# Gated cross-attention and feed-forward on one core: two head pairs per attention step in place of one

## What is computed

```python
def xattn(x, context):                      # x is layer-normed before
    q = split_heads(x @ Wq) * 64 ** -0.5
    k, v = map(split_heads, split(context @ Wkv))
    k, v = concat(null_kv[0], k), concat(null_kv[1], v)   # one null key, value
    out = merge_heads(softmax(q @ k.T) @ v) @ Wout
    return layernorm(out, eps=1e-6) * ln_scale + ln_bias
x = x + tanh(g_xattn) * xattn(layernorm(x), ctx)
x = x + tanh(g_ffn) * ffn(layernorm(x))     # gated, quantised over whole tensors
```

## Time and profile before

| what | value |
|---|---|
| median of three executions | 598.54 us |
| the profiled execution, its own time | 599.63 us |
| its span in the trace | 597.6 us |
| busy: PE, PE's weight loads, DVE, ACT, POOL | 524.0, 456.4, 410.5, 298.4, 123.6 us |
| group 0, and each of groups 1 to 5 | 50.10 us |
| group 6 | 42.01 us |
| group 7, to the start of its W | 33.16 us |
| from the end of W to the end of the kernel | 166.2 us |

### The profile page before, as it was taken

One profiled execution on the slowest core, in us unless ns is written; L12 is line 12 of the kernel. 1 busy time (PEld: TensorE's weight loads), 2 busy tenths in 40 slices (PEclk: granted clock), 3 DMA queues, 4 the chain that ended last, 5 costly groups with the idle time before them and its releaser, 6 DMA issues. The chain is left out here.

```text
span 597.6 us, 10965 instructions
## 1 busy us (share of the span) xinstructions
PE 524.0 (88%) x3921; PEld 456.4 (76%) x3921; DVE 410.5 (69%) x1077; ACT 298.4 (50%) x858; POOL 123.6 (21%) x137
## 2 busy tenths in 40 slices
PE   2999999999999999999999999997639999500997
PEld 2988889888988988888898898885528888400996
DVE  4779744754764574575476458658748989999685
ACT  3635532632542362363254335327325569897773
POOL 3001301220221130122022112213031029900000
PEclk9999999999999999999999999999959999855799
DMA  7922001101100110110110001005001000100033
GB/s 257 361 88 72 1 1 54 37 1 54 35 0 0 53 35 0 53 35 0 35 45 8 1 2 36 2 1 160 0 19 35 2 0 1 35 1 1 1 106 105
DMA packets 18478, 25.86 MB, mean 43 GB/s; under 512 B 1216, under 2 KB 15808, under 8 KB 18448
## 3 DMA queue, kind: packets, MB, share of 16 engines
q1 hardware_dynamic: 18192, 25.17, 12.8%
q0 software_dynamic: 256, 0.30, 0.2%
HBM read 21.27 MB, written 4.19 MB: 43 GB/s over the span
## 5 line engine op out<-in xcount | busy, mean ns | idle before, releaser
L804 ACT ACTIVATE probs<-bank,nmax 128x129 f32<-128x129 f32 x256 | 90.9, 368 | 117.8 <-DVE nmax L1132 117.7
L1551 POOL TENSOR_TENSOR probs<-probs,rinv 128x512 f32<-128x512 f32 x64 | 66.7, 1042 | 337.8 <-DVE rinv L1140 337.8
L607 PE MATMUL bank<-wv,ctxT 128*128 128x512 f32 x384 | 94.2, 397 | 0.0
L599 PE MATMUL bank<-ctxT,wk 128*128 128x256 f32 x672 | 88.9, 282 | 0.0
L599 PEld LDWEIGHTS bank<-ctxT,wk 128*128 128x128 f32 x672 | 83.6, 188 | 0.0
L607 PEld LDWEIGHTS bank<-wv,ctxT 128*128 128x128 f32 x384 | 70.5, 188 | 16.9 <-issue 1.2
L1144 DVE COPY pT<-bank 128x512 f32<-128x512 f32 x64 | 43.7, 682 | 20.7 <-PE bank L670 18.7
L599 PE MATMUL bank<-xnT,wq 128*128 128x256 f32 x336 | 54.7, 298 | 0.0
L785 ACT ACTIVATE oT<-bank 128x256 fp32r<-128x256 f32 x64 | 24.7, 386 | 60.0 <-PE bank L679 60.0
L804 ACT ACTIVATION_READ_ACCUMULATOR probs<-bank,nmax 128x1 f32 x256 | 52.0, 203 | 0.0
L599 PEld LDWEIGHTS bank<-xnT,wq 128*128 128x128 f32 x336 | 43.2, 188 | 7.2 <-issue 1.2
(11 more groups left out here) (170 smaller groups left out, 810.6 us busy)
## 6 DMA issues: line engine op xcount, KB each, us to landing
craw<-in_ctx SPq DMA_DIRECT2D x8, 512.0 KB, 3.3
stage<-in_L_xattn_Wkv SPq DMA_DIRECT2D x8, 512.0 KB, 11.9
xa<-in_x SPq DMA_DIRECT2D x8, 256.0 KB, 2.7
xr<-in_x SPq DMA_DIRECT2D x8, 256.0 KB, 2.8
x_scratch<-y SPq DMA_DIRECT2D x7, 256.0 KB, 2.1
x2all<-x_scratch SPq DMA_DIRECT2D x1, 1792.0 KB, 8.3
xres<-x_scratch SPq DMA_DIRECT2D x6, 256.0 KB, 2.8
out<-yout SPq DMA_DIRECT2D x6, 256.0 KB, 2.2
```

What stands on the lines that cost most here:

```text
L599: last = mm(bk[:, n * TG:(n + 1) * TG], wt[a][:, k, f], act_t[b][:, k, :], start=(k == 0 and i == 0), stop=(k == kk - 1 and i == len(TERMS ...
L607: last = mm(bk[:, :], ctxT[a][:, k, b * S:(b + 1) * S], wv[w][:, k, h * 512:(h + 1) * 512], start=(k == 0 and i == 0), stop=(k == KC - 1 a ...
L804: last = nc.scalar.activation(probs[:, c % 2, u, 0:NK], score_bank[c % 2][h][:, b * QW:b * QW + NK], ACT.Exp, bias=nmax[:, c % 2, u:u + 1] ...
L1551: G.tensor_tensor(probs[:, c % 2, :, 0:S], probs[:, c % 2, :, 0:S], rinv[:, c % 2, :].rearrange("p (u o) -> p u o", o=1).to_broadcast([P, ...
```

## The change

The eight steps become four (PAIRS = NS // 2), each with two head pairs 2p and 2p+1.

- PE: scores of both head pairs of the next step stand back to back at its head, in all four score banks; then prob_transposes(2p), the units of plan step 2p, prob_transposes(2p+1), the units of plan step 2p+1, and then the values of both, into all 512 columns of pv_bank. In the last group the second scores stand ahead of prob_transposes(2p+1).
- out_high and out_low take 512 columns at once, once in a step.
- DVE: both maxima stand at the head of the step; then for each head pair the other work (now beside(c)), prob_copy, inverse_sums, unit evacuations; out_low at the end of the step. attention_stats no longer has a maxima in its middle.
- ACT: exps of one head pair ahead of each of the two sets of unit evacuations, out_high at the end.
- The prologue makes scores, maxima and exps of head pairs 0 and 1 of group 0; POOL normalises two there.
- ot_lo and pv_done count steps of two (g * PAIRS + p).

```diff
--- before.py
+++ after.py
@@ -642,7 +643,7 @@
                         o = bank[0][:, 0:D] if last_group and b else bk[:, b * D:(b + 1) * D]
                         mm(o, mean[:, :], wc[:, :], start=True, stop=False)
                         if b == 0:
-                            wait(pe, ot_lo, g * NS + NS)
+                            wait(pe, ot_lo, g * PAIRS + PAIRS)
                         for k in range(KF):
                             for i, (a, w) in enumerate(TERMS):
                                 last = mm(o, oT[a][:, k, b * S:(b + 1) * S], wout[w][:, k, :],
@@ -670,14 +671,16 @@
                     last = nc.tensor.transpose(pt_bank[:, u * P:(u + 1) * P], probs[:, c % 2, u, 0:S], ident[:, :])
                 last.then_inc(pt_done, 1)
 
-            def values(g, c):
-                wait(pe, pt_copied, g * NS + c + 1)
-                wait(pe, ot_lo, g * NS + c)
-                for b in range(GB):
-                    for h in range(2):
-                        rows = slice(h * DH, (h + 1) * DH)
-                        last = mm(pv_bank[rows, b * S:(b + 1) * S], v[:, b, c, rows],
-                                  pT[:, c % 2, 2 * h + b, :], start=True, stop=True)
+            def values(g, p):
+                wait(pe, pt_copied, g * NS + 2 * p + 2)
+                wait(pe, ot_lo, g * PAIRS + p)
+                for n in range(2):
+                    c = 2 * p + n
+                    for b in range(GB):
+                        for h in range(2):
+                            rows = slice(h * DH, (h + 1) * DH)
+                            last = mm(pv_bank[rows, n * TG + b * S:n * TG + (b + 1) * S], v[:, b, c, rows],
+                                      pT[:, n, 2 * h + b, :], start=True, stop=True)
                 last.then_inc(pv_done, 1)
 
             for pos in range(len(PRO)):
@@ -685,22 +688,25 @@
                 if PRO[pos] == "k6":
                     pe.wait_ge(null_ready, 1)
                     scores(0, 0)
+                    scores(0, 1)
 
             def group(g):
                 final = isinstance(g, int) and g == NG - 1
                 pos, (steps, tail) = 0, plan(g)
-                for c in range(NS):
-                    if c + 1 < NS:
-                        scores(g, c + 1)
-                    for _ in steps[c]:
-                        unit(g, pos)
-                        pos += 1
-                    prob_transposes(g, c)
-                    if c:
-                        values(g, c - 1)
-                if not final:
-                    scores(g + 1, 0)
-                values(g, NS - 1)
+                for p in range(PAIRS):
+                    to = (g, 2 * p + 2) if p + 1 < PAIRS else (None if final else (g + 1, 0))
+                    if to:
+                        scores(to[0], to[1])
+                        if not final:
+                            scores(to[0], to[1] + 1)
+                    for n in range(2):
+                        if n and to and final:
+                            scores(to[0], to[1] + 1)
+                        prob_transposes(g, 2 * p + n)
+                        for _ in steps[2 * p + n]:
+                            unit(g, pos)
+                            pos += 1
+                    values(g, p)
                 for u in tail:
                     if u != "C":
                         unit(g, pos)
@@ -806,9 +812,10 @@
                                                 bias=nmax[:, c % 2, u:u + 1], accum_out=rowsum[:, c % 2, u:u + 1])
                 last.then_inc(exp_done, 1)
 
-            def out_high(g, c):
-                wait(act, pv_done, g * NS + c + 1)
-                high(oT[0][:, c, :], pv_bank[:, 0:TG]).then_inc(ot_hi, 1)
+            def out_high(g, p):
+                wait(act, pv_done, g * PAIRS + p + 1)
+                high(oT[0][:, 2 * p:2 * p + 2, :],
+                     pv_bank[:, :].rearrange("p (c s) -> p c s", c=2)).then_inc(ot_hi, 1)
 
             def ctx_high(n, units_before):
                 act.wait_ge(ctx_in, (n + 1) * 16)
@@ -831,6 +838,7 @@
                 split("pro", npos[0])
                 if PRO[npos[0]] == "k6":
                     exps(0, 0)
+                    exps(0, 1)
                 if PRO[npos[0]] == "V11":
                     ctx_high(1, PRO.index("V11") + 1)
                 npos[0] += 1
@@ -838,21 +846,15 @@
             def group(g):
                 final = isinstance(g, int) and g == NG - 1
                 pos, (steps, tail) = 0, plan(g)
-                for c in range(NS):
-
-                    weights = steps[c][0][0:1] == "F"
-                    if c + 1 < NS and not weights:
-                        exps(g, c + 1)
-                    for _ in steps[c]:
-                        split(g, pos)
-                        pos += 1
-                    if c + 1 < NS and weights:
-                        exps(g, c + 1)
-                    if c:
-                        out_high(g, c - 1)
-                if not final:
-                    exps(g + 1, 0)
-                out_high(g, NS - 1)
+                for p in range(PAIRS):
+                    to = (g, 2 * p + 2) if p + 1 < PAIRS else (None if final else (g + 1, 0))
+                    for n in range(2):
+                        if to:
+                            exps(to[0], to[1] + n)
+                        for _ in steps[2 * p + n]:
+                            split(g, pos)
+                            pos += 1
+                    out_high(g, p)
                 for u in tail:
                     if u == "C":
                         ctx_high(g + 2, units(g)[1] + BODY.index("V11") + 1)
@@ -1078,7 +1080,6 @@
                 for b in range(GB):
                     last = V.bn_stats(bn[:, 2 + b, :], bk[:, b * D:(b + 1) * D])
                 ln2.count(last)
-                maxima(g + 1, 1)
                 ln2.wait()
                 settle()
                 for b in range(GB):
@@ -1144,9 +1145,10 @@
                 V.tensor_copy(pT[:, c % 2, :, :],
                               pt_bank[:, :].rearrange("p (u s) -> p u s", u=4)).then_inc(pt_copied, 1)
 
-            def out_low(g, c):
-                dve.wait_ge(ot_hi, g * NS + c + 1)
-                low(oT[1][:, c, :], pv_bank[:, 0:TG], oT[0][:, c, :]).then_inc(ot_lo, 1)
+            def out_low(g, p):
+                dve.wait_ge(ot_hi, g * PAIRS + p + 1)
+                low(oT[1][:, 2 * p:2 * p + 2, :], pv_bank[:, :].rearrange("p (c s) -> p c s", c=2),
+                    oT[0][:, 2 * p:2 * p + 2, :]).then_inc(ot_lo, 1)
 
             def weight_scales(m):
 
@@ -1202,8 +1204,10 @@
             while npos[0] < len(PRO):
                 if PRO[npos[0]] == "V00":
                     ln_stats(1)
+                    inverse_sums(0, 0)
                 elif PRO[npos[0]] == "V10":
                     ln_rstd()
+                    inverse_sums(0, 1)
                 elif PRO[npos[0]] == "V01":
                     ln_apply()
                 elif PRO[npos[0]] == "V11":
@@ -1213,21 +1217,18 @@
                 split("pro", npos[0])
                 if PRO[npos[0]] == "k6":
                     maxima(0, 0)
-                    inverse_sums(0, 0)
+                    maxima(0, 1)
                 if PRO[npos[0]] == "V11":
                     ctx_low(1)
                 npos[0] += 1
 
-            maxima(0, 1)
             dve.wait_ge(const_ready, 1)
 
             def group(g):
                 peeled, final = isinstance(g, int), isinstance(g, int) and g == NG - 1
                 first = peeled and g == 0
                 pos, (steps, tail) = 0, plan(g)
-                for c in range(NS):
-                    if 1 <= c < NS - 1:
-                        maxima(g, c + 1)
+                def beside(c):
 
                     if c == 1 and not first:
                         attention_rstd(g - 1)
@@ -1247,25 +1248,23 @@
                         (weight_scales, weight_integers, weight_values)[c - 1](1)
                     if peeled and g == NG - 2 and 4 <= c < 7:
                         (weight_scales, weight_integers, weight_values)[c - 4](2)
-                    weights = steps[c][0][0:1] == "F"
-                    if c < NS - 1 and not weights:
-                        inverse_sums(g, c + 1)
-                    if c == NS - 1:
+                for p in range(PAIRS):
+                    to = (g, 2 * p + 2) if p + 1 < PAIRS else (None if final else (g + 1, 0))
+                    if to and not final:
+                        maxima(to[0], to[1])
+                        maxima(to[0], to[1] + 1)
+                    for n in range(2):
+                        c = 2 * p + n
+                        if to and final:
+                            maxima(to[0], to[1] + n)
+                        beside(c)
                         prob_copy(g, c)
-                        out_low(g, c - 1)
-                    for _ in steps[c]:
-                        split(g, pos)
-                        pos += 1
```

(21 more changed lines are left out.)

## The result

The changed kernel took 608.44 us (median of four executions, 607.02 to 611.04), the kernel before 599.03: a ratio of 1.015, 95% interval 1.0125 to 1.0175. The forecast was 603.0 us, slower, in a range of 593 to 611. The sign was right and the time lies in the range, but the loss is 9.4 us where 4.5 was forecast against the median.

A forecast was written before the change was run, and what follows sets the result against it. PE was taken as the bound, busy 49.71 of 50.10 us in a loop group. Saving 18.1, then +4.0 (group 0), 5 x 2.85, +5.8 (group 6), -1.3 (group 7) gave +4.6 us: 603 us, range 593 to 611.

The forecast's parts named there:

- What is saved: Loop groups: fewer changes of array shape on PE, 2.2 us, and no 0.39 us wait for out_low; 2.6 a group.
- The price of a change of shape: PE switching between whole-array, row-tiled and column-tiled work: 0.15 us into values, about 0.20 otherwise, also assumed for scores to transposes.
- What becomes late: prob_transposes(2p+1) waits for prob_copy(2p), queued on DVE behind out_low, both maxima and beside(2p); PE stalls by beside - 0.32 us.
- rival A: Faster: the copy comes in time despite DVE's order, all of 18.1 + 1.3 us gained, 579 us; chance 0.08 whole, 0.12 half.
- the sum of 2.85 us of stalls: Loop group PE stalls: 1.84 us at c = 2, 0.63 at c = 4, none at c = 6, 0.38 at c = 0.
- The odd halves have slack: Odd head pairs' copies cause no stall: prob_copy(3) follows x2_statistics at 7.7 us, and values want it at 8.2.
- are read a step later: ACT's exponentials need 1.54 us after the maxima and are read only a step later.
- Rival B: Slower still: odd halves late as well, DVE operations stretching 0.5 to 1 us a group, +4 to +7, 609 us; joint chance 0.18.
- With waits of 1.4 us the clock stayed at 1.00: Profile before: PE's granted clock held through 1.4 us waits; none of the new group waits was to exceed 2.6 us.
- The reserve named for a drop: If the clock dropped: at most group 7's 27 us of PE work at half speed over its gaps, some 6 us.
- rival D: Where PE stalls at prob_transposes(2p+1), savings ahead from back-to-back scores only lengthen the stall; slower, joint chance 0.18.
- the walk: Step-by-step count of PE and DVE times from a step's first scores, putting the copy 0.3 to 2.2 us late.

The follow-up runs named there:

- the control: The changed kernel run once more, unedited, for its spread and a second profile: 609.14 us, ratio 1.017 to the kernel before.

## Why the prediction was right in sign and short in size

- What is saved (2.6 us a group, 18.1 over seven) was right. Without waits a loop group takes 47.42 us; 50.10 less the forecast 2.6 is 47.5. The price of a change of shape was a little high for transposes after scores (0.41 us for 0.54), which the trace of before did not have.
- What becomes late, and why, was right: the copy of the even head pair behind attention_norm, ln_stats and the weight work. Moving the copy ahead of it, with nothing else changed, turned 1.5% slower into 2.7% faster, 582.45 us, near the 579 of rival A.
- **The step that failed** is the sum of 2.85 us of stalls for a loop group. It measured 3.7 (group 3 has 51.16 us, not 50.35, and 47.42 without waits). Half of the 0.8 missing is a term put at nothing: "The odd halves have slack" was worked out at c = 3 and not at c = 1. There attention_rstd ran 0.89 us longer beside POOL's normalise, behind 0.39 us in which VectorE waited for ScalarE, and values(0) waited some 0.4 us; the run without both gave back 0.42 us a group. The sentence that the exponentials "are read a step later" has no place for that wait of 0.39 us: the reciprocal of their sums stands in the same half step. The rest is arithmetic: the copy reaches PE 0.15 us after its end (at c = 3 it ended at 216.42 + 0.68, and PE started at 217.25), not 0.06, at three places a group, and ln_stats took 1.06 us, not 0.95.
- Of the 6.8 us that the profiled execution is over the forecast, groups 1 to 5 make 3.9 (+5.1 for +1.25). Group 6 makes 1.8, of which 1.56 is the clock: in the control, where it stayed at 1.00, the group has 45.48 us, +3.5 for the forecast +3.2. Group 7 makes 0.9.
- Rival B had the kind of the error (DVE operations stretched, odd halves late, +4 to +7, 609 us) and looked for it at c = 3; it was at c = 1. The trace of before had the sign: weight_integers took 2.50 us from 371.22 on, and POOL's addition to xr ran there until 372.10; after the change it took 1.73, since there it started first and POOL's operation was the one that became longer (last section).

```profile
370.81 1.29 POOL L1562 TENSOR_TENSOR xr<-xr,gb 128x512 f32<-128x512 f32 x1
```

- "With waits of 1.4 us the clock stayed at 1.00" did not carry to waits of 2.1. The reserve named for a drop (at most 6 us) was kept out of the sum. In group 6 a drop cost 1.56 us in one of the two profiles of the changed kernel; in group 7 the clock fell in both, and the group gained 0.2 to 0.4 us, not 1.3. How much of that is the clock's was not separated.
- That none of the saving in back-to-back scores survives where PE stalls behind them (rival D) is in the walk, whose 5.59 us for the transposes at c = 3 measured 5.64; no run tested it by itself.

## What to carry to other kernels

This is one kernel's experience. When work on the busiest engine is batched, look at what the next engine has queued between the first and the last consumer of the batch: a single buffer (here pt_bank) emptied by an in-order queue sets the pace, and the emptying belongs at the head of that queue. Ask of each wait removed where the work ahead of it goes next; one order changed at one place gained 0.8 us for a wait of 1.9, the same order changed throughout gained 3.2 (51.15 to 47.97, with 47.42 for no wait at all). On VectorE look at the duration of small operations that start as GpSimd starts.

## What the runs showed that was not expected

- VectorE and GpSimd hold each other up even where VectorE touches two columns: 1.06 us in place of 0.17, to the end of the other's operation; at another place 0.65, again to its end. It goes the other way too. In group 6 of the changed kernel VectorE's weight_integers started 0.17 us ahead of GpSimd's normalise, and the normalise took 2.46 us in place of 1.04:

```profile
379.87 1.73 DVE L1167 TENSOR_TENSOR fint<-fraw,fs 128x1536 int16<-128x1536 f32 x1
```

```profile
380.04 2.46 POOL L1550 TENSOR_TENSOR probs<-probs,rinv 128x512 f32<-128x512 f32 x1 [4.96 <-DVE rinv L1141]
```

  Not every operation meets this: prob_copy out of the bank (206.28 in the run with the reciprocal later, 0.69 us) and the statistics of y (217.12 here, 0.42 us) lay beside a normalise and kept their durations. The Trainium skill (SBUF — State Buffer, SBUF: two separate sides) calls the port pair of the two engines an exclusive lock that the loser waits for through the whole instruction, for VectorE operations in a two-port mode or with two inputs there. The rows agree in that one of the two is held until the other ends; in which mode the two-column operations ran, no trace shows.
- The granted clock fell to its lower level for part of a 3.6 us stretch (mean 0.57) about a wait of 2.1 us in one execution, and not in another with the same wait; in loop groups with waits up to 1.8 us it was 1.00 throughout. What decides between the two executions stays open; the 1.56 us between their groups 6 is part of the spread of the changed kernel (607.0 to 611.0).
- Transposes after row-tiled scores cost little more than the exit from the scores. From the first score of a head pair to the first transpose pass 0.65 us (195.16 to 195.81 with the scores apart), as many as to Q's first matmul before the change (49.48 to 50.13); the transposes themselves then take 0.05 us longer than behind a unit (0.41 for 0.36).
